# Two conditioned feed-forward layers: new layout and queue order for the inputs, basis products ahead of the weight's transpositions

## The chip, the cores and the metric

The kernel runs on one core of one Trainium2 chip. The metric is the device time of one execution in microseconds (us); three runs of the kernel before gave 230.68, 230.73 and 230.92, median 230.73. Engines are called by the profile's names: PE is TensorE (PEld its weight loads), DVE is VectorE, ACT ScalarE, POOL GpSimd, SP SyncE.

## The reference

Two layers, each a per-sample channel mixing followed by a feed-forward product and a residual sum. `x` is 128 samples of 32 channels by 512.

```python
def mixed(x, kind, weights):            # weights[kind]: 32x32 for each sample
    return jnp.einsum('bct,bcd->bdt', x, weights[kind])

# layer 0
base = einsum('bsd,od->bso', y, W_base) + b_base
e0, e1 = einsum('bsd,rd->bsr', y, enc0), einsum('bsd,rd->bsr', y, enc1)      # ranks 32 and 8
w0, w1 = coefs0 * mask0, coefs1 * mask1                                      # 3 experts, [3, 512, rank]
decoded = einsum('bsr,eor->ebso', e0, w0) + einsum('bsr,eor->ebso', e1, w1)
update = real_fourier_orthogonal_multiply(decoded).sum(axis=0)               # an inverse real FFT
x = x + base + update * 0.5
# layer 1
x = x + scale * einsum('bsi,if->bsf', y, kernel * 2.0 - 1.0)
```

## The kernel before

A tile is four samples, 128 partitions of 512 columns; there are 32 tiles. Layer 0's base weight, encoder, decoder and Fourier basis are folded into one 512x512 matrix before the first tile. This stage ahead of the loop is what the change touches.

- The masked coefficients of the three experts are multiplied and summed on DVE (`masked`, `pair`, `decode`).
- PE multiplies `decode` with the even and odd halves of the Fourier basis (`basis_sb`, line 426), into `y1_ps` (odd) and `f1_ps` (even). ACT and DVE make `spectrum` out of the two.
- PE transposes the base weight `w_sb` into the four PSUM banks `a_ps` (`turn_w`, line 414: 16 transpositions of 128x128, eight per half), and adds the products of encoder and spectrum there (line 488).
- ACT and DVE split each bank into `a_high` and `a_low`.
- POOL computes the gather's indices from `row_of` (DVE, from `kinds`), gathers each sample's mixing rows, and ACT expands them into block diagonals (`blocks`, line 277).
- Then 32 tiles run through a software pipeline: mixing product (line 432), feed of layer 0 (452, 462), mixing, feed of layer 1 (469, 474), with residual sums on DVE and the bias on POOL.

Every engine runs its own program in the order in which it is written, and semaphores join them. Loads are issued by SP and ACT (hardware queues q1 and q10 in the profile) and POOL (software queue q0), each queue in the order of its issues. The weight comes in two halves, one from SP, one from ACT. Before the first real product PE runs products of a zero tile (`warm_up`, line 407), ten, and two more after the first eight transpositions.

Of the kernel before, what the change touches and what calls it, by code (L numbers as in the profile page):

```python
# [23 lines left out]
P = 128  # L24
SAMPLES, C, T = 128, 32, 512
PER_TILE = P // C
TILES = SAMPLES // PER_TILE
CHUNKS = T // P
KINDS0, KINDS1 = 16, 32
EXPERTS, R0, R1 = 3, 32, 8  # L30
R = R0 + R1
HALF = T // 2 + 1
SCALING = 16.0 / 32.0
LAYERS = 2
# [20 lines left out]
    return np.ascontiguousarray(f.reshape(P, CHUNKS // 2, 2, HALF).transpose(2, 0, 1, 3).astype(np.float32))  # L55


def build(nc, x, kind0, kind1, mix0, w_base, b_base, enc0, enc1, coefs0, coefs1, mask0, mask1,
          mix1, sign_bits, scale, basis, out):
    f32, f32r, u8 = mybir.dt.float32, mybir.dt.float32r, mybir.dt.uint8  # L60
    i32, u32 = mybir.dt.int32, mybir.dt.uint32
    ALU, ACT = mybir.AluOpType, mybir.ActivationFunctionType
# [7 lines left out]
    with ctx:  # L70
        def sb(name, shape, dt):
            return ctx.enter_context(nc.sbuf_tensor(name, shape, dt))
# [4 lines left out]
        def sem(name):  # L77
            return ctx.enter_context(nc.semaphore(name))


        kinds = sb("kinds", [P, LAYERS, SAMPLES], i32)
        channel = sb("channel", [P, 1], i32)
        partition = sb("partition", [P, 1], i32)
        row_of = sb("row_of", [P, TILES, LAYERS], i32)
# [4 lines left out]
        w_sb = sb("w_sb", [P, CHUNKS, T], f32)  # L89
        basis_sb = sb("basis_sb", [P, 2, CHUNKS // 2, HALF], f32)  # L90

        coefs_sb = sb("coefs_sb", [P, EXPERTS, CHUNKS * R], f32)
        masks_sb = sb("masks_sb", [P, EXPERTS, CHUNKS * R], u8)
# [4 lines left out]
        enc_sb = sb("enc_sb", [P, T], f32)  # L98
# [30 lines left out]
        kinds_loaded, partition_ready, channel_ready, row_of_ready = (  # L129
            sem("kinds_loaded"), sem("partition_ready"), sem("channel_ready"), sem("row_of_ready"))  # L130
        blocks_zero, idle_zero = sem("blocks_zero"), sem("idle_zero")
        w_loaded = [sem(f"w_loaded{half}") for half in range(2)]
        basis_loaded = [sem(f"basis_loaded{parity}") for parity in range(2)]
        coefs_loaded, masks_loaded = sem("coefs_loaded"), sem("masks_loaded")
        enc_loaded, bits_loaded, bias_loaded, scale_loaded = (
            sem("enc_loaded"), sem("bits_loaded"), sem("bias_loaded"), sem("scale_loaded"))
        ident_zero, ident_ready = sem("ident_zero"), sem("ident_ready")
# [19 lines left out]


        def load_w(queue, half):
            part = slice(half * T // 2, (half + 1) * T // 2)  # L160
            queue.dma_start(w_sb[:, :, part], w_base.rearrange("(c p) d -> p c d", p=P)[:, :, part]).then_inc(w_loaded[half], 16)

        @block.sync
        def _(sp):
            sp.dma_start(kinds[:, 0, :], kind0.partition_broadcast(P)).then_inc(kinds_loaded, 16)  # L165
            load_w(sp, 0)
            sp.dma_start(coefs_sb[:, :, CHUNKS * R0:], coefs1.rearrange("e (p q) r -> p e (q r)", q=CHUNKS)).then_inc(coefs_loaded, 16)
            sp.dma_start(basis_sb[:, 1], basis[1]).then_inc(basis_loaded[1], 16)
            sp.wait_ge(enc_zero, 1)
            sp.dma_start(enc_sb[0:R0, :], enc0).then_inc(enc_loaded, 16)  # L170
            sp.dma_start(enc_sb[R0:R, :], enc1).then_inc(enc_loaded, 16)
            sp.dma_start(bias[:, :], b_base.partition_broadcast(P)).then_inc(bias_loaded, 16)
            sp.dma_start(x_in[:, 1, :], x_tiles[1]).then_inc(x_loaded[1], 16)
            sp.dma_start(bits_sb[:, :, :], sign_bits.rearrange("(c p) f -> p c f", p=P)).then_inc(bits_loaded, 16)
            sp.dma_start(scale_sb[:, :], scale.partition_broadcast(P)).then_inc(scale_loaded, 16)
            sp.dma_start(x_in[:, 2, :], x_tiles[2]).then_inc(x_loaded[2], 16)

            def load(tile, slot):
                sp.wait_ge(mixed0, tile - RING + 1)
                sp.wait_ge(biased, tile - RING + 1)  # L180
                sp.dma_start(x_in[:, slot, :], x_tiles[bass.ds(tile, 1)].rearrange("a p t -> (a p) t")
                             ).then_inc(x_loaded[slot], 16)

            def store(tile, slot):
                sp.wait_ge(out_ready, tile + 1)
                sp.dma_start(out_tiles[bass.ds(tile, 1)].rearrange("a p t -> (a p) t"), x1[:, slot, :]
                             ).then_inc(stored[slot], 16)

            looped = (TILES - RING) // RING * RING
            with sp.Fori(0, looped, RING) as base:  # L190
                for u in range(RING):
                    load(base + u + RING, u)
                    store(base + u, u)
            for tile in range(looped, TILES - 1):
                if tile + RING < TILES:
                    load(tile + RING, tile % RING)
                store(tile, tile % RING)
            for half, columns in enumerate(halves):
                sp.wait_ge(out_ready, TILES + half)
                sp.dma_start(out_tiles[TILES - 1][:, columns], x1[:, (TILES - 1) % RING, columns]).then_inc(ended, 16)  # L200

            for slot in range(RING):
                sp.wait_ge(stored[slot], 16 * len(range(slot, TILES - 1, RING)))
            sp.wait_ge(ended, 32)

        @block.gpsimd
        def _(pool):
            pool.dma_start(masks_sb[:, :, 0:CHUNKS * R0], mask0.rearrange("e (p q) r -> p e (q r)", q=CHUNKS)).then_inc(masks_loaded, 16)
            pool.dma_start(masks_sb[:, :, CHUNKS * R0:], mask1.rearrange("e (p q) r -> p e (q r)", q=CHUNKS)).then_inc(masks_loaded, 16)
            nc.gpsimd.iota(partition[:, :], pattern=[[0, 1]], base=0, channel_multiplier=1).then_inc(partition_ready, 1)  # L210

            nc.gpsimd.memset(ident[:, :], 0.0).then_inc(ident_zero, 1)
# [32 lines left out]
                if more:  # L245
                    gather(row_now[:, slot, :], slot)

            pool.wait_ge(row_of_ready, PER_TILE)
            gather(row_of[:, 0, :], 0)
            for slot in range(1, RING):  # L250
                gather(row_of[:, slot, :], slot)
# [8 lines left out]

        @block.scalar
        def _(act):
            act.dma_start(kinds[:, 1, :], kind1.partition_broadcast(P)).then_inc(kinds_loaded, 16)
            act.dma_start(coefs_sb[:, :, 0:CHUNKS * R0], coefs0.rearrange("e (p q) r -> p e (q r)", q=CHUNKS)).then_inc(coefs_loaded, 16)
            act.dma_start(basis_sb[:, 0], basis[0]).then_inc(basis_loaded[0], 16)
            load_w(act, 1)
            act.dma_start(x_in[:, 0, :], x_tiles[0]).then_inc(x_loaded[0], 16)
# [46 lines left out]
        def _(dve):  # L314
# [4 lines left out]
            dve.wait_ge(partition_ready, 1)  # L319
            nc.vector.tensor_scalar(channel[:, :], partition[:, :], C - 1, None, ALU.bitwise_and).then_inc(channel_ready, 1)  # L320
            dve.wait_ge(channel_ready, 1)
            dve.wait_ge(kinds_loaded, 16 * LAYERS)
            for j in range(PER_TILE):
                part = slice(j * C, (j + 1) * C)
                nc.vector.tensor_scalar(row_of[part, :, :].rearrange("p n l -> p l n"), kinds[part, :, j::PER_TILE], float(C), channel[part, :],
                                        ALU.mult, ALU.add).then_inc(row_of_ready, 1)

            dve.wait_ge(coefs_loaded, 32)
            dve.wait_ge(masks_loaded, 32)
            nc.vector.tensor_tensor(out=masked[:, :, :], in0=coefs_sb[:, :, :], in1=masks_sb[:, :, :], op=ALU.mult).then_inc(masked_ready, 1)  # L330
            dve.wait_ge(masked_ready, 1)
            nc.vector.tensor_tensor(out=pair[:, :], in0=masked[:, 0, :], in1=masked[:, 1, :], op=ALU.add).then_inc(pair_ready, 1)
# [2 lines left out]
            for first, rank, at in ((0, R0, 0), (CHUNKS * R0, R1, R0)):  # L335
                part = slice(first, first + CHUNKS * rank)
                nc.vector.tensor_tensor(out=decode[:, :, at:at + rank], in0=pair[:, part].rearrange("p (q r) -> p q r", r=rank),
                                        in1=masked[:, 2, part].rearrange("p (q r) -> p q r", r=rank), op=ALU.add).then_inc(decode_ready, 1)

            dve.wait_ge(odd_ready, 1)  # L340
            nc.vector.tensor_scalar(constant2[:, :], odd_part[:, 0:1], 2.0, None, ALU.mult).then_inc(constant_ready, 1)
# [60 lines left out]
        def _(pe):  # L402

            pe.wait_ge(idle_zero, 1)
            def warm_up(count):
                for _ in range(count):
                    nc.tensor.matmul(f0_ps[:, :], idle[:, 0:P], idle[:, :], start=True, stop=True)  # L407


            def turn_w(half):  # L410
                pe.wait_ge(w_loaded[half], 16)
                for k in (2 * half, 2 * half + 1):
                    for c in range(CHUNKS):
                        nc.tensor.matmul(a_ps[k][:, c * P:(c + 1) * P], w_sb[:, c, k * P:(k + 1) * P], ident[:, :],  # L414
                                         start=(c == 0), stop=False, is_transpose=True, skip_group_check=True)

            warm_up(10)
            pe.wait_ge(ident_ready, 1)
            turn_w(0)
            warm_up(2)  # L420

            pe.wait_ge(decode_ready, 2)
            for parity, to, done in ((0, odd_ps, odd_done), (1, even_ps, even_done)):
# [47 lines left out]
            def feed1_low(count, to=f1_ps[:, :], columns=slice(0, T)):  # L471
# [3 lines left out]
                                            start=False, stop=(k == CHUNKS - 1))  # L475
                last.then_inc(fed1, 1)

            turn_w(1)

            pe.wait_ge(enc_loaded, 32)  # L480
            for k in range(CHUNKS):
                if k == FIRST_MIX:
                    mix0_tile(0, 0, 0)
# [39 lines left out]
                feed1_low(TILES, end_ps[half], halves[half])  # L523


INPUTS = ["x", "itok_B_0_15", "itok_B_0_30", "L0_cond_weights", "L0_ffn_W_base", "L0_ffn_b_base", "L0_ffn_enc0",
          "L0_ffn_enc1", "L0_ffn_coefs0", "L0_ffn_coefs1", "L0_ffn_mask0", "L0_ffn_mask1", "L1_cond_weights",
          "L1_ffn_kernel", "L1_ffn_scale"]


# [13 lines left out]
```

## Time and profile before

| | |
|---|---|
| median of three runs | 230.73 us |
| span of the profiled execution | 229.0 us |
| time around the span, median less span | 1.7 us |
| PE busy | 221.5 us, 97% |
| DVE, ACT, POOL busy | 99.7, 75.1, 111.6 us |
| chain that ended last | PE 95%, DMA 3% |

The profiled execution has no time of its own but its span; 1.7 us is the distance of the median to it. A span is from the first to the last instruction. A busy share says how much of the span an engine's instructions took; the chain that ended last says what the end waited for, step by step.

### The profile page before, as it was taken

The numbers are of one execution on the slowest core, as the hardware profiler recorded it, in microseconds if no ns is written. First come the engines' busy times: TensorE is split into PE (matmuls) and PEld (weight loads), VectorE is DVE, ScalarE is ACT, GpSimd is POOL, SyncE is SP. The second block draws the span as 40 slices with busy tenths as digits, with TensorE's granted clock in tenths as the row PEclk, the third lists the DMA queues.
The fourth block names the chain that finished last, engine by engine and source line by source line (L and its number), as shares of the span: only waits on it lengthen the run. The fifth ranks groups of instructions, "written<-read, shape, count | busy, mean of one in ns | idle before, by whom it ended". The sixth has DMA issues, their size and how long they took to land.

```text
span 229.0 us, 3592 instructions
## 1 busy us (share of the span) xinstructions
PE 221.5 (97%) x1206; PEld 185.7 (81%) x1206; DVE 99.7 (44%) x150; ACT 75.1 (33%) x199; POOL 111.6 (49%) x135
## 2 busy tenths in 40 slices
PE   7499999999999999999999999999999999999995
PEld 2376888888888888888888888888888888888884
DVE  2325634434343434434343434434344444434334
ACT  0228433322333233322333333322333333322211
POOL 5466834555545444555545445555545444522200
PEclk9999999999999999999999999999999999999999
DMA  2972032123323322223322331223323232123112
GB/s 43 315 254 52 9 93 72 69 66 94 97 94 97 97 80 73 78 67 94 97 95 97 97 94 58 77 69 94 97 94 97 97 88 71 69 67 92 46 46 93
DMA packets 14789, 20.51 MB, mean 90 GB/s; under 512 B 2808, under 2 KB 6280, under 8 KB 14784
## 3 DMA queue, kind: packets, MB, share of 16 engines
q1 hardware_dynamic: 11312, 18.03, 24.6%
q0 software_dynamic: 2112, 1.11, 2.4%
q10 hardware_dynamic: 1360, 1.31, 2.0%
q8 instruction: 2, 0.03, 0.1%
q14 instruction: 3, 0.02, 0.0%
HBM read 12.06 MB, written 8.39 MB: 89 GB/s over the span
## 4 chain that ended last, share of the span: by engine, by line
PE 95%; DMA 3%; DVE 0%; issue 0%; SPq 0%
PE f_ps L452 26%; PE y_ps L432 25%; PE f_ps L462 13%; PE f_ps L474 13%; PE f_ps L469 13%; DMA w_sb<-in_L_ffn_W_base 3%; PE a_ps L488 2%; PE a_ps L414 1%; PE y_ps L426 1%; DVE x L398 0%; PE a_ps L469 0%; PE f_ps L426 0%; PE f_ps L407 0%; PE a_ps L474 0%; SPq L165 0%
## 5 line engine op out<-in xcount | busy, mean ns | idle before, releaser
L228 POOL TENSOR_TENSOR x<-x_in,bias 128x512 f32<-128x512 f32 x32 | 40.8, 1275 | 81.1 <-issue 46.6
L221 POOL DMA_INDIRECT gathered<-in_L_cond_weights,row_now x58 | 56.5, 973 | 13.2 <-issue 9.2
L452 PE MATMUL f_ps<-a_high,y_high 128*128 128x512 f32 x128 | 53.5, 418 | 0.0
L452 PE MATMUL f_ps<-a_low,y_high 128*128 128x512 f32 x128 | 50.4, 394 | 0.0
L364 DVE TENSOR_TENSOR x<-f_ps,x 128x512 f32<-128x512 f32 x32 | 22.1, 692 | 49.7 <-PE f_ps L452 48.1
L290 ACT ACTIVATE y_high<-y_ps 128x512 fp32r<-128x512 f32 x32 | 19.1, 597 | 69.4 <-PE y_ps L432 69.4
L286 ACT ACTIVATE y_high<-y_ps 128x512 fp32r<-128x512 f32 x32 | 19.1, 597 | 61.7 <-PE y_ps L432 59.7
L469 PE MATMUL f_ps<-b_sign,y_high 128*128 128x512 f32 x124 | 36.3, 414 | 0.0
L432 PEld LDWEIGHTS y_ps<-blocks,x_in 128*128 128x128 f32 x256 | 33.5, 191 | 3.3 <-issue 0.5
L432 PEld LDWEIGHTS y_ps<-blocks,x 128*128 128x128 f32 x256 | 33.3, 191 | 3.2 <-DVE x L364 0.5
L462 PE MATMUL f_ps<-a_high,y_low 128*128 128x512 f32 x128 | 35.0, 394 | 0.0
L277 ACT ACTIVATE blocks<-gathered 32x64 f32<-32x64 f32 x128 | 32.6, 255 | 4.5 <-issue 1.4
L474 PE MATMUL f_ps<-b_sign,y_low 128*128 128x512 f32 x124 | 34.0, 396 | 0.0
L432 PE MATMUL y_ps<-blocks,x 128*128 128x128 f32 x256 | 33.9, 275 | 0.0
L432 PE MATMUL y_ps<-blocks,x_in 128*128 128x128 f32 x256 | 33.7, 275 | 0.0
L357 DVE TENSOR_TENSOR y_low<-y_ps,y_high 128x512 fp32r<-128x512 f32 x32 | 22.1, 692 | 25.3 <-ACT y_high L290 23.0
L352 DVE TENSOR_TENSOR y_low<-y_ps,y_high 128x512 fp32r<-128x512 f32 x32 | 22.1, 692 | 23.0 <-ACT y_high L286 23.0
L370 DVE SCALAR_TENSOR_TENSOR x<-f_ps,scale_sb,x 128x512 f32<-128x512 f32 x31 | 23.3, 751 | 16.2 <-PE f_ps L474 15.7
L462 PEld LDWEIGHTS f_ps<-a_high,y_low 128*128 128x128 f32 x128 | 23.9, 187 | 5.9
L452 PEld LDWEIGHTS f_ps<-a_high,y_high 128*128 128x128 f32 x128 | 24.1, 188 | 4.7 <-issue 0.2
L452 PEld LDWEIGHTS f_ps<-a_low,y_high 128*128 128x128 f32 x128 | 24.1, 188 | 4.7 <-issue 0.2
L474 PEld LDWEIGHTS f_ps<-b_sign,y_low 128*128 128x128 f32 x124 | 23.2, 188 | 5.5
(46 smaller groups left out, 78.3 us busy)
## 6 DMA issues: line engine op xcount, KB each, us to landing
x_in<-in_x SPq DMA_DIRECT2D x31, 256.0 KB
out_x<-x SPq DMA_DIRECT2D x31, 256.0 KB, 2.0
gathered<-in_L_cond_weights,row_now POOLq DMA_INDIRECT x58
w_sb<-in_L_ffn_W_base SPq DMA_DIRECT2D x1, 512.0 KB
w_sb<-in_L_ffn_W_base ACTq DMA_DIRECT2D x1, 512.0 KB
basis_sb<-in_fourier_basis ACTq DMA_DIRECT2D x1, 257.0 KB
basis_sb<-in_fourier_basis SPq DMA_DIRECT2D x1, 257.0 KB
x_in<-in_x ACTq DMA_DIRECT2D x1, 256.0 KB
```

Of the source, the lines that this page charges most:

```text
L221: nc.gpsimd.indirect_dma_start(gathered[:, slot, layer, :], None, mix_rows[layer], IndirectOffsetOnAxis(rows[:, layer:layer + 1].bitcast(u ...
L228: nc.gpsimd.tensor_tensor(out=x1[:, slot, :], in0=x_in[:, slot, :], in1=bias[:, :], op=ALU.add).then_inc(biased, 1)
L277: nc.scalar.activation(blocks[part, slot, :, part], gathered[part, slot, :, :], ACT.Copy).then_inc(expanded, 1)
L352: nc.vector.tensor_tensor(out=y0_low[:, :], in0=y0_ps[:, :], in1=y0_high[:, :].bitcast(f32), op=ALU.subtract).then_inc(y0_low_ready, 1)
L357: nc.vector.tensor_tensor(out=y1_low[:, :], in0=y1_ps[:, :], in1=y1_high[:, :].bitcast(f32), op=ALU.subtract).then_inc(y1_low_ready, 1)
L364: nc.vector.tensor_tensor(out=x1[:, slot, :], in0=f0_ps[:, :], in1=x1[:, slot, :], op=ALU.add).then_inc(x1_ready, 1)
L370: nc.vector.scalar_tensor_tensor(out=x1[:, slot, :], in0=f1_ps[:, :], scalar=scale_sb[:, 0:1], in1=x1[:, slot, :], op0=ALU.mult, op1=ALU.a ...
L432: last = nc.tensor.matmul(to[:, k * P:(k + 1) * P], of[:, k * P:(k + 1) * P], blocks[:, slot, layer, :], start=True, stop=True)
L452: last = nc.tensor.matmul(f0_ps[:, :], y0_high[:, k * P:(k + 1) * P], a[:, k, :], start=(k == 0 and a is a_high), stop=(k == CHUNKS - 1 an ...
L462: nc.tensor.matmul(f0_ps[:, :], y0_low[:, k * P:(k + 1) * P], a_high[:, k, :], start=False, stop=False)
L469: nc.tensor.matmul(to, y1_high[:, k * P:(k + 1) * P], b_sign[:, k, columns], start=(k == 0), stop=False)
L474: last = nc.tensor.matmul(to, y1_low[:, k * P:(k + 1) * P], b_sign[:, k, columns], start=False, stop=(k == CHUNKS - 1))
```

## The change

Host-side, the two sets of coefficients and masks become one array each, laid out so that every partition reads one contiguous row; the two encoders become one array, and the kinds become an array by partition, [128, 32, 2], with each sample's kind repeated for its 32 channels. So the two coefficient DMAs, two mask DMAs, two encoder DMAs and two kinds DMAs become one each. The halves of the base weight are by rows (output chunks) and not by columns. The queues' order changes. On PE, the idle products are 18 and run together, the basis products come next, and all sixteen transpositions after them. The numbers in the kernel's lines above are of the kernel before.

```diff
-            part = slice(half * T // 2, (half + 1) * T // 2)
-            queue.dma_start(w_sb[:, :, part], w_base.rearrange("(c p) d -> p c d", p=P)[:, :, part]).then_inc(w_loaded[half], 16)
+            part = slice(2 * half, 2 * half + 2)
+            queue.dma_start(w_sb[:, part, :], w_base.rearrange("(c p) d -> p c d", p=P)[:, part, :]).then_inc(w_loaded[half], 16)
@@ SP
-            sp.dma_start(kinds[:, 0, :], kind0.partition_broadcast(P)).then_inc(kinds_loaded, 16)
+            sp.dma_start(coefs_sb[:, :, :], coefs).then_inc(coefs_loaded, 16)
+            sp.dma_start(basis_sb[:, 1], basis[1]).then_inc(basis_loaded[1], 16)
             load_w(sp, 0)
-            sp.dma_start(coefs_sb[:, :, CHUNKS * R0:], coefs1.rearrange("e (p q) r -> p e (q r)", q=CHUNKS)).then_inc(coefs_loaded, 16)
-            sp.dma_start(basis_sb[:, 1], basis[1]).then_inc(basis_loaded[1], 16)
             sp.wait_ge(enc_zero, 1)
-            sp.dma_start(enc_sb[0:R0, :], enc0).then_inc(enc_loaded, 16)
-            sp.dma_start(enc_sb[R0:R, :], enc1).then_inc(enc_loaded, 16)
+            sp.dma_start(enc_sb[0:R, :], enc).then_inc(enc_loaded, 16)
@@ POOL
-            pool.dma_start(masks_sb[:, :, 0:CHUNKS * R0], mask0.rearrange("e (p q) r -> p e (q r)", q=CHUNKS)).then_inc(masks_loaded, 16)
-            pool.dma_start(masks_sb[:, :, CHUNKS * R0:], mask1.rearrange("e (p q) r -> p e (q r)", q=CHUNKS)).then_inc(masks_loaded, 16)
@@ ACT
-            act.dma_start(kinds[:, 1, :], kind1.partition_broadcast(P)).then_inc(kinds_loaded, 16)
-            act.dma_start(coefs_sb[:, :, 0:CHUNKS * R0], coefs0.rearrange("e (p q) r -> p e (q r)", q=CHUNKS)).then_inc(coefs_loaded, 16)
+            act.dma_start(kinds[:, :, :], kinds_in).then_inc(kinds_loaded, 16)
+            act.dma_start(masks_sb[:, :, :], masks).then_inc(masks_loaded, 16)
@@ DVE
-            for j in range(PER_TILE):
-                part = slice(j * C, (j + 1) * C)
-                nc.vector.tensor_scalar(row_of[part, :, :].rearrange("p n l -> p l n"), kinds[part, :, j::PER_TILE], float(C), channel[part, :],
-                                        ALU.mult, ALU.add).then_inc(row_of_ready, 1)
+            nc.vector.tensor_scalar(row_of[:, :, :], kinds[:, :, :], float(C), channel[:, :], ALU.mult, ALU.add).then_inc(row_of_ready, 1)
@@ PE
-                for k in (2 * half, 2 * half + 1):
-                    for c in range(CHUNKS):
+                for k in range(CHUNKS):
+                    for c in (2 * half, 2 * half + 1):
-            warm_up(10)
-            pe.wait_ge(ident_ready, 1)
-            turn_w(0)
-            warm_up(2)
+            warm_up(18)
...
+            pe.wait_ge(ident_ready, 1)
+            turn_w(0)
             turn_w(1)
-            pe.wait_ge(enc_loaded, 32)
+            pe.wait_ge(enc_loaded, 16)
```

PE before, from its first product to the encoder's last (`f0_ps<-idle` are the idle products, `y1_ps` and `f1_ps` the basis products, `a_ps<-ident,w_sb` the transpositions):

```order
L407 MATMUL f0_ps<-idle 128x512 x10
L414 MATMUL a_ps0<-ident,w_sb 128x128 x4
L414 MATMUL a_ps1<-ident,w_sb 128x128 x4
L407 MATMUL f0_ps<-idle 128x512 x2
L426 MATMUL y1_ps<-basis_sb,decode 128x257 x2
L426 MATMUL f1_ps<-basis_sb,decode 128x257 x2
L414 MATMUL a_ps2<-ident,w_sb 128x128 x4
L414 MATMUL a_ps3<-ident,w_sb 128x128 x4
L488 MATMUL a_ps0<-spectrum,enc_sb 128x257
```

PE now, the same stretch:

```order
L401 MATMUL f0_ps<-idle 128x512 x18
L417 MATMUL y1_ps<-basis_sb,decode 128x257 x2
L417 MATMUL f1_ps<-basis_sb,decode 128x257 x2
L408 MATMUL a_ps0<-ident,w_sb 128x128 x2
L408 MATMUL a_ps1<-ident,w_sb 128x128 x2
L408 MATMUL a_ps2<-ident,w_sb 128x128 x2
L408 MATMUL a_ps3<-ident,w_sb 128x128 x2
...
L481 MATMUL a_ps0<-spectrum,enc_sb 128x257
```

The basis products moved ahead of all transpositions, and each half of the weight now fills two chunks of all four banks, where it filled two banks whole.

SP's queue before, its first loads (shapes are partitions by elements of a row):

```order
L165 DMA kinds<-in_itok_B_15 128x128
L161 DMA w_sb<-in_L_ffn_W_base 128x4x256
L167 DMA coefs_sb<-in_L_ffn_coefs 128x3x32
L168 DMA basis_sb<-in_fourier_basis 128x514
L170 DMA enc_sb<-in_L_ffn_enc 32x512
L171 DMA enc_sb<-in_L_ffn_enc 8x512
L172 DMA bias<-in_L_ffn_b_base 128x512
```

SP's queue now:

```order
L165 DMA coefs_sb<-in_coefs 128x480
L166 DMA basis_sb<-in_fourier_basis 128x514
L161 DMA w_sb<-in_L_ffn_W_base 128x2x512
L169 DMA enc_sb<-in_enc 40x512
L170 DMA bias<-in_L_ffn_b_base 128x512
```

The coefficients and the basis moved ahead of SP's half of the weight, and the kinds left this queue.

ACT's queue now (before it was kinds, the larger part of the coefficients, basis, weight, x):

```order
L259 DMA kinds<-in_kinds 128x64
L260 DMA masks_sb<-in_masks 128x480
L261 DMA basis_sb<-in_fourier_basis 128x514
L161 DMA w_sb<-in_L_ffn_W_base 128x2x512
L263 DMA x_in<-in_x 128x512
```

The masks came here from POOL's software queue, and the coefficients went to SP.

## Rows read from the trace of the kernel before

**Rows 1.** The page: span, PE's busy time, shares of the last chain.

```profile
span 229.0 us, 3592 instructions
PE 221.5 (97%) x1206; PEld 185.7 (81%) x1206; DVE 99.7 (44%) x150; ACT 75.1 (33%) x199; POOL 111.6 (49%) x135
PE 95%; DMA 3%; DVE 0%; issue 0%; SPq 0%
```

**Rows 2.** Busy us (instructions) by stretch: PE, PEld, DVE, ACT, POOL; clock, DMA share, GB/s.

```profile
190.00:209.50 19.50, 19.50 (x110) 16.77 (x109) 8.48 (x12) 6.80 (x19) 7.71 (x8) 1.00 0.28 85
```

**Rows 3.** The last chain before the loop: start us, us, what.

```profile
1.20 7.50 DMA w_sb<-in_L_ffn_W_base
9.01 1.94 PE a_ps L414 x8
10.95 0.85 PE f_ps L407 x2
11.80 1.95 PE y_ps L426 x4
13.75 0.93 PE f_ps L426 x4
14.82 1.09 PE a_ps L414 x8
15.91 1.73 PE a_ps L488 x6
17.64 0.89 PE y_ps L432 x8
```

**Rows 4.** Timeline of PE: start us, us, instructions, idle before and releaser.

```profile
1.21 4.45 PE L407 MATMUL f_ps<-idle 128*128 128x512 bf16 x10 [1.21 <-DVE idle L315]
9.01 1.94 PE L414 MATMUL a_ps<-ident,w_sb 128*128 128x128 f32 x8 [3.35 <-DMA w_sb<-in_L_ffn_W_base]
```

**Rows 5.** Timeline of POOL's first mask DMA and DVE's instructions around it.

```profile
1.29 0.93 POOL L208 DMA_DIRECT2D masks_sb<-in_L_ffn_mask  x1 [0.83 <-POOLq L535]
10.17 0.66 DVE L330 TENSOR_TENSOR masked<-coefs_sb,masks_sb 128x480 f32<-128x480 f32 x1 [2.04 <-DMA masks_sb<-in_L_ffn_mask]
11.22 0.39 DVE L337 TENSOR_TENSOR decode<-pair,masked 128x128 f32<-128x128 f32 x2
15.14 0.41 DVE L348 SCALAR_TENSOR_TENSOR spectrum<-f_ps,mirrored 128x255 f32<-128x255 f32 x1
```

**Rows 6.** Timeline of row_of, the first gather and its expansion.

```profile
6.97 1.17 DVE L325 TENSOR_SCALAR row_of<-kinds,channel 32x64 int32<-32x64 int32 x4 [3.55 <-DMA kinds<-in_itok_B]
8.41 1.03 POOL L221 DMA_INDIRECT gathered<-in_L_cond_weights,row_of  x1 [4.11 <-DVE row_of L325]
15.55 1.09 ACT L277 ACTIVATE blocks<-gathered 32x64 f32<-32x64 f32 x4 [1.38 <-issue]
```

**Rows 7.** Busy time by stretch, before and after 5.5 us.

```profile
0.00:5.50 5.50, 4.29 (x10) 1.34 (x10) 1.61 (x4) 0.02 (x1) 2.97 (x10) 1.00 0.21 38
5.50:15.00 9.50, 6.01 (x21) 4.21 (x21) 3.16 (x11) 1.86 (x3) 5.07 (x6) 1.00 1.07 324
```

**Rows 8.** DMA queues (packets, MB, share), windows 0:5.5, 0:8, 0:13; the kinds' landing (us).

```profile
q1 hardware_dynamic: 214, 0.15, 12.5%
q10 hardware_dynamic: 124, 0.06, 8.8%
...
q1 hardware_dynamic: 912, 0.63, 28.2%
...
q1 hardware_dynamic: 1633, 1.54, 40.3%
q10 hardware_dynamic: 1162, 1.04, 29.2%
q0 software_dynamic: 64, 0.06, 1.4%
...
kinds<-in_itok_B ACTq DMA_DIRECT2D x1, 64.0 KB, 5.0
```

More of the change, by code:

```diff
@@ L55, in fourier_basis, with build @@
     return np.ascontiguousarray(f.reshape(P, CHUNKS // 2, 2, HALF).transpose(2, 0, 1, 3).astype(np.float32))
-def build(nc, x, kind0, kind1, mix0, w_base, b_base, enc0, enc1, coefs0, coefs1, mask0, mask1,
+def build(nc, x, kinds_in, mix0, w_base, b_base, enc, coefs, masks,
           mix1, sign_bits, scale, basis, out):
@@ L78, in sem @@
             return ctx.enter_context(nc.semaphore(name))
-        kinds = sb("kinds", [P, LAYERS, SAMPLES], i32)
+        kinds = sb("kinds", [P, TILES, LAYERS], i32)
         channel = sb("channel", [P, 1], i32)
@@ L246, in prepare @@
                     gather(row_now[:, slot, :], slot)
-            pool.wait_ge(row_of_ready, PER_TILE)
+            pool.wait_ge(row_of_ready, 1)
             gather(row_of[:, 0, :], 0)
@@ L321, in _ @@
             dve.wait_ge(channel_ready, 1)
-            dve.wait_ge(kinds_loaded, 16 * LAYERS)
-            for j in range(PER_TILE):
-                part = slice(j * C, (j + 1) * C)
-                nc.vector.tensor_scalar(row_of[part, :, :].rearrange("p n l -> p l n"), kinds[part, :, j::PER_TILE], float(C), channel[part, :],
-                                        ALU.mult, ALU.add).then_inc(row_of_ready, 1)
-            dve.wait_ge(coefs_loaded, 32)
-            dve.wait_ge(masks_loaded, 32)
+            dve.wait_ge(kinds_loaded, 16)
+            nc.vector.tensor_scalar(row_of[:, :, :], kinds[:, :, :], float(C), channel[:, :], ALU.mult, ALU.add).then_inc(row_of_ready, 1)
+            dve.wait_ge(coefs_loaded, 16)
+            dve.wait_ge(masks_loaded, 16)
             nc.vector.tensor_tensor(out=masked[:, :, :], in0=coefs_sb[:, :, :], in1=masks_sb[:, :, :], op=ALU.mult).then_inc(masked_ready, 1)
@@ L523, in _, with by_partition, kinds_by_partition @@
                 feed1_low(TILES, end_ps[half], halves[half])
-INPUTS = ["x", "itok_B_0_15", "itok_B_0_30", "L0_cond_weights", "L0_ffn_W_base", "L0_ffn_b_base", "L0_ffn_enc0",
-          "L0_ffn_enc1", "L0_ffn_coefs0", "L0_ffn_coefs1", "L0_ffn_mask0", "L0_ffn_mask1", "L1_cond_weights",
-          "L1_ffn_kernel", "L1_ffn_scale"]
+INPUTS = ["x", "kinds", "L0_cond_weights", "L0_ffn_W_base", "L0_ffn_b_base", "enc", "coefs", "masks",
+          "L1_cond_weights", "L1_ffn_kernel", "L1_ffn_scale"]
+def by_partition(per_rank0, per_rank1):
+    sides = [np.asarray(a).reshape(EXPERTS, P, -1) for a in (per_rank0, per_rank1)]
+    return np.concatenate(sides, axis=2).transpose(1, 0, 2)
+def kinds_by_partition(kind0, kind1):
+    both = np.stack([np.asarray(k).reshape(TILES, PER_TILE) for k in (kind0, kind1)], axis=2)
+    return np.repeat(both.transpose(1, 0, 2), C, axis=0)
 def kernel(**inputs):
@@ L535 @@
     nc = bacc.Bacc("TRN2", target_bir_lowering=False, num_devices=1)
+    inputs["kinds"] = kinds_by_partition(inputs["itok_B_0_15"], inputs["itok_B_0_30"])
+    inputs["enc"] = np.concatenate([inputs["L0_ffn_enc0"], inputs["L0_ffn_enc1"]])
+    inputs["coefs"] = by_partition(inputs["L0_ffn_coefs0"], inputs["L0_ffn_coefs1"])
+    inputs["masks"] = by_partition(inputs["L0_ffn_mask0"], inputs["L0_ffn_mask1"])
     arrays = {name: np.ascontiguousarray(inputs[name]) for name in INPUTS}
```

## The prediction

> **What bounds the kernel now.** I read the page first. PE is busy 97% of the span, the chain that ended last is 95% PE and 3% one DMA [rows 1]. A stretch late in the loop has PE busy for 19.50 of 19.50 us [rows 2], so the 31 steps of the main loop have no gap, and this change touches none of their instructions. What can move the end is the stage before the loop, and a microsecond saved on PE there should arrive at the end whole. So I read that stage in the chain, in order of time [rows 3]: a DMA until 8.70 (half 0 of the base weight), then PE alone. The first eight transpositions take 1.94 us, two idle products 0.85, the four pieces of the odd basis product 1.95, the even ones 0.93, the other eight transpositions 1.09, then the encoder products, the first mixing product and feed.
>
> Then the inputs of each step. PE ran ten idle products from 1.21 to 5.66 and then rested until 9.01 for the weight [rows 4]. VectorE waited 2.04 us for the masks, which landed at 10.17 though GpSimd had issued them at 1.29; masked, pair and decode end at 11.61 [rows 5]. So the basis product could not start before about 11.7 in any case: the weight and then the masks bound this stretch. The kinds reached VectorE at 6.97, the gathers were issued from 8.41 and ScalarE could expand the first only at 15.55 [rows 6]. The DMA engines moved 38 GB/s up to 5.5 us, 324 GB/s from there to 15 [rows 7], and the two hardware queues' shares are in [rows 8].
>
> The span, 229.0 us, is of one execution; the median of the timed runs is 230.73, so 1.7 us lie around the span. I add up in the span and carry the difference over to the median. About 0.2% (0.46 us) is what a measurement of this kernel can tell from no change.
>
> **The change, part by part.** The new order on PE is 18 idle products, basis products, sixteen transpositions, encoder. The encoder products began in the chain at 15.91 [rows 3]; the question is when the sixteen transpositions end now, and how far ahead of 15.91 that is.
>
> *Idle products.* Ten ran 1.21 to 5.66, 0.427 us apart by two of them in 0.85 us [rows 3, 4]. Eighteen at that pace end at 1.21 + 7.7 = 8.9. PE's clock shows in the same rows: eight transpositions took 1.94 us and later eight took 1.09, the odd basis product 1.95 and the even one 0.93 [rows 3]. The slower of each pair is at 1.2 GHz, the faster at 2.4, and the clock rose around 13.7, after PE had worked on from 9.01. (The granted clock prints as 1.00 in the early window too [rows 7]; the durations tell more.) With unbroken work from 1.21 I expect it to rise between 5.7, which it had not done in ten, and 8; if it rises at 6.9, 13 products are done and the other five take half of 2.1, so the 18 end at 7.9. Bounds: 7.9 and 8.9.
>
> *Decode.* Masks and coefficients are now one contiguous row per partition, first in the queues. On SP 0.246 MB of coefficients, 0.263 of basis, 0.524 of weight: 1.033 MB. On ACT 0.033 kinds, 0.061 masks, 0.263 basis, 0.524 weight: 0.881 MB, then x. From 5.5 to 13 q1 moved 1.39 MB, 0.185 per us, and q10 0.98 MB, 0.131 per us [rows 8]. Half 0 of the weight, which ends at 0.59 MB on q1 behind the kinds, passed about 7.8 (0.63 MB by 8.0), was seen landed at 8.70, and PE started at 9.01 [rows 3, 8]: 0.9 from bytes to landing, 1.2 to PE. Now two bounds. Slow start: as before, only 0.15 and 0.06 MB by 5.5. Then the coefficients are through at 6.0, the masks at 5.8, decode inputs at 6.9; masked to decode took 10.17 to 11.61, 1.44 us [rows 5], so decode at 8.4, and basis 0 at 5.5 + 0.30/0.131 + 0.9 = 8.7. Fast start: the full rates from 2.0 (an estimate: SP issued its weight at 1.20 [rows 3], and something passes before bytes move), so decode some 3 us sooner. Either way the odd basis product starts at 8 to 9, not 11.7, and with the clock up both end near 10 to 10.9 (0.93 + 0.93 after 8.1 to 9.0). The spectrum followed the even product's end (14.68) by 0.86, at 15.55; now it is ready by 11.8, in the shadow of the transpositions, so it costs nothing; if the transpositions were to end before it, it would cost the difference. The two idle products between (0.85) are gone from the path.
>
> *The weight.* It now stands behind the basis. Slow: SP's half through at 5.5 + 0.883/0.185 = 10.3, at PE 11.5; ACT's at 5.5 + 0.82/0.131 = 11.8, at PE 13.0. The first eight transpositions hide in the wait for the second half; the last eight end at 13.0 + 1.09 = 14.1. Fast: 0.65 and 0.46 MB are through by 5.5, SP's half is at PE 8.8, ACT's at 9.9; PE, free at 9.8, does sixteen in 2.18 and ends at 12.0. So the encoder starts 1.8 us sooner (slow) to 3.9 us sooner (fast). Which end? Up to 5.5 the rows show 214 and 124 packets [rows 8], most of them the kinds, where 128 partitions read one row of 512 B. The new kernel starts with a row for each partition, of 256 to 2056 B. If packets were the limit, as many of the new ones carry about 0.45 MB where the old ones carried 0.21; if the shared row was, the start is fast. I take the middle of the two ends, 2.9 us.
>
> *The rest.* Encoder data are one DMA for two, behind SP's weight: 0.08 MB, 0.4 us, hidden by the transpositions. Four row_of instructions of 0.27 become one; kinds were on VectorE at 6.97 and POOL's gather started at 8.41. Now the kinds are a quarter as many bytes on one queue; 5.0 us to landing was the better of the two before [rows 8], so row_of at 5.8 and gather at 6.4 (1.44 behind the kinds before, with 0.9 of it the three instructions saved). The first gather took 15.55 − 8.41 = 7.1 us to expand, so 13.5 now, expanded at 14.6. It is wanted by the mixing product 1.73 us after the encoder starts, 14.7 to 15.8: just hidden. x is wanted at the same place; ACT's queue reaches its end at 1.143 MB, slow 13.8, landed 14.7: hidden. POOL loses two DMA issues, the first of 0.93 [rows 5], and zeroes the encoder tile earlier; SP waits for that before it issues the encoder, bias, x and bits, none of which is near its deadline. Everything from the encoder on keeps its distances. Sum: 229.0 − 2.9 = 226.1 in the span, about 230.7 − 2.9 = **227.9 us**.
>
> **The rivals.** *Queues at full rate from the start* (15%): the rows before don't show a start without the shared rows, so it can't be excluded. Gain 3.9: 226.9. For it: the first DMA of ACT's queue was 64 KB and took 5.0 us to land [rows 8], at 38 GB/s in all where later 324 were moved [rows 7]. DMA: Bandwidth & Descriptors (the Trainium skill, section on the anatomy of one DMA) gives about 2.0 us plus bytes over 436 GB/s for one; by that formula 64 KB take some 2.2 us, where this trace has 5.0, and the kernel would be at the fast end, so the trace disagrees with it as it stands.
>
> *The gathers bind* (12%). By 13.0 q0 had moved 0.06 MB, no more than the masks' 60 KB [rows 8], though the first gather had been issued at 8.41 [rows 6]: its bytes came with the end of the bulk. If they still come only then and ScalarE expands from 15.55, done at 16.64 [rows 6], the mixing product starts at 16.7 where it stood at 17.64: gain 0.9, 229.8. In part of these cases they come half a microsecond sooner: 229.3.
>
> *The clock falls in the wait for the weight* (10%), the way to the other side. PE has finished the basis products by 10 to 10.9 and rests up to 11.5 and again before 13.0. After the 3.35 us of rest before it worked at 1.2 GHz from 9.01 to 13.7 [rows 3, 4]. If the same happens here, 4.7 us of work go at half speed and 2.35 us are lost: 227.9 becomes 230.2, and from the slow end 231.3. It makes the kernel slower as soon as the second half reaches PE after 12.5 (12.5 + 1.09 + 2.35 = 15.9). Against it: these rests are some 1 us and 0.4 us, and nothing in the trace shows a clock that fell once it was up. TensorE: Matmul & The Clock Gate (the Trainium skill, on oscillation) warns of bursts separated by waits on DMAs, each starting cold; no row here shows such a fall.
>
> *The change gives nothing* (5%): its gain is eaten elsewhere before the loop, for instance by ScalarE's evictions of a_high: 230.7.
>
> **How the numbers follow.** Main case 58% (its own range 227.1 to 229.0, the bounds of the weight), fast start 15%, gathers 12%, clock 10% of which half slower, nothing 5%. The range 226.7 to 229.5 leaves out the clock case, no gain and the worse gathers, under 2 in 10. Faster: 58 + 15 + 12 + 3 = 88%; same 7%; slower 5%.
>
> **What would show it.** The idle products end at 7.9 to 8.9 with a halved pace at the end; decode ready by 8.5, the odd basis product from 8 to 9 in 0.93; a wait of PE for w_sb of 0.5 to 2 us, then transpositions at 1.09 for eight; encoder 12.0 to 14.1; the loop's stretches still at 19.50 of 19.50. Wrong would make me: transpositions at 1.94, a mixing product that waits for blocks, or a loop with gaps because x or its stores come too late.

## The result, and the profile after

The changed kernel takes 227.69 us (227.64 to 228.27 in four runs) against 230.82 before in the same runs; the ratio is 0.986, 95% interval 0.984 to 0.988. The forecast was 227.9, with a range of 226.7 to 229.5. The span fell by 3.5 us, from 229.0 to 225.5; the time by 3.1, since what lies around the span (median less span) grew from 1.8 to 2.2 us.

The page of the changed kernel, to be held against [rows 1]: the span, PE's busy time, and the last chain, by line.

```profile
span 225.5 us, 3597 instructions
PE 220.1 (98%) x1212; PEld 185.2 (82%) x1212; DVE 98.8 (44%) x147; ACT 75.0 (33%) x199; POOL 110.1 (49%) x133
PE f_ps L443 26%; PE y_ps L423 26%; PE f_ps L453 13%; PE f_ps L460 13%; PE f_ps L465 13%; DMA basis_sb<-in_fourier_basis 3%; PE a_ps L481 2%; PE a_ps L408 1%; PE y_ps L417 0%; DVE x L392 0%; PE a_ps L460 0%; PE f_ps L417 0%; PE a_ps L465 0%; ACTq L260 0%; ACTq L259 0%
```

PE is still the chain; the one DMA in it is now the basis, not the weight, and PE never waits for the weight. The chain before the loop (start us, us, what), the counterpart of [rows 3]:

```profile
1.67 6.68 DMA basis_sb<-in_fourier_basis
8.35 0.14 issue
8.49 1.11 PE y_ps L417 x4
9.60 0.87 PE f_ps L417 x4
10.47 1.75 PE a_ps L408 x16
12.21 1.73 PE a_ps L481 x6
13.94 1.08 PE y_ps L423 x8
15.02 1.72 PE a_ps L481 x4
```

The encoder products start at 12.21 where they stood at 15.91: 3.70 us. The first mixing product, behind them, takes 1.08 us where it took 0.89, so 3.5 are left. They reach the end, since the loop is as tight as before (the busy time of a late stretch, as in [rows 2]):

```profile
190.00:209.50 19.50, 19.50 (x110) 16.80 (x109) 8.64 (x13) 6.50 (x18) 5.77 (x5) 1.00 0.26 86
```

The timeline of what stands ahead of the basis products, as in [rows 4, 5, 6]:

```profile
1.20 5.87 PE L401 MATMUL f_ps<-idle 128*128 128x512 bf16 x18 [1.20 <-DVE idle L311]
3.91 0.26 DVE L319 TENSOR_SCALAR row_of<-kinds,channel 128x64 int32<-128x64 int32 x1 [1.40 <-DMA kinds<-in_kinds]
4.45 1.11 POOL L217 DMA_INDIRECT gathered<-in_L_cond_weights,row_of  x1 [2.40 <-DVE row_of L319]
4.74 0.66 DVE L323 TENSOR_TENSOR masked<-coefs_sb,masks_sb 128x480 f32<-128x480 f32 x1 [0.58 <-DMA masks_sb<-in_masks]
5.80 0.39 DVE L330 TENSOR_TENSOR decode<-pair,masked 128x128 f32<-128x128 f32 x2
8.49 1.11 PE L417 MATMUL y_ps<-basis_sb,decode 128*128 128x257 f32 x4 [1.42 <-DMA basis_sb<-in_fourier_basis]
12.66 1.09 ACT L273 ACTIVATE blocks<-gathered 32x64 f32<-32x64 f32 x4 [2.64 <-DMA gathered<-in_L_cond_weights,row_of]
```

VectorE has the kinds at 3.9 us (before: 7.0) and `decode` is ready at 6.2 (before: 11.6). The idle products end at 7.07, and PE then rests 1.42 us for the basis half in ACT's queue, which the odd product needs. The first gather is issued 4 us sooner, but ScalarE starts to expand its rows only 2.9 us sooner and is done at 13.75, two tenths ahead of the product that wants them. The queues in the window 0:5.5 (packets, MB, share), against the first two of [rows 8]:

```profile
q1 hardware_dynamic: 436, 0.81, 47.6%
q10 hardware_dynamic: 378, 0.28, 15.5%
```

They moved 1.09 MB by 5.5 us where the kernel before moved 0.21.

### The profile page after: what moved, and what is told of

It reads as the page before. It is cut to its first block, busy times and chain, and to the rows that moved or that the text cites. A ratio compares the mean times of both kernels' runs of the same rounds, so it can differ in the third digit from the quotient of the medians.

```text
span 225.5 us, 3597 instructions
## 1 busy us (share of the span) xinstructions
PE 220.1 (98%) x1212; PEld 185.2 (82%) x1212; DVE 98.8 (44%) x147; ACT 75.0 (33%) x199; POOL 110.1 (49%) x133
## 4 chain that ended last, share of the span: by engine, by line
PE 95%; DMA 3%; DVE 0%; ACTq 0%; issue 0%
PE f_ps L443 26%; PE y_ps L423 26%; PE f_ps L453 13%; PE f_ps L460 13%; PE f_ps L465 13%; DMA basis_sb<-in_fourier_basis 3%; PE a_ps L481 2%; PE a_ps L408 1%; PE y_ps L417 0%; DVE x L392 0%; PE a_ps L460 0%; PE f_ps L417 0%; PE a_ps L465 0%; ACTq L260 0%; ACTq L259 0%
```

## The experiments

The open questions were which edit ended the slow start, whether PE's order or the loads bring the gain, and what the idle products are for. Times are medians; the kernel before, measured beside each group, had 230.97 to 231.09. Line numbers in rows are each kernel's own.

**Only the kinds new.** The kernel before, with the kinds' array by partition, and with it the one `row_of` instruction for four:

```diff
-            sp.dma_start(kinds[:, 0, :], kind0.partition_broadcast(P)).then_inc(kinds_loaded, 16)
...
-            act.dma_start(kinds[:, 1, :], kind1.partition_broadcast(P)).then_inc(kinds_loaded, 16)
+            act.dma_start(kinds[:, :, :], kinds_in).then_inc(kinds_loaded, 16)
```

> The kernel before with only the kinds changed: one array with a row of 256 bytes for each partition, loaded by ACT, one row_of instruction; SP starts with its half of the weight. Theory (the shared rows of the kinds make the slow start): 0.6 MB or more by 5.5 us in place of 0.21, SP's weight landed near 6.5 in place of 8.7, masks and decode 1 to 2 us sooner, time 229 to 229.8. Rival (the slow start has another cause, such as the masks in the software queue or the many short rows): near 0.3 MB by 5.5 and 230.5 or more.

Measured: 228.92 us (227.86 to 230.02), ratio 0.990, interval 0.985 to 0.995. Queues in the window 0:5.5, then the timeline of DVE and PE, then busy time by stretch (the third number from the end is the granted clock):

```profile
q1 hardware_dynamic: 936, 0.59, 35.5%
q10 hardware_dynamic: 664, 0.46, 25.3%
q0 software_dynamic: 16, 0.03, 1.8%
...
8.21 0.66 DVE L326 TENSOR_TENSOR masked<-coefs_sb,masks_sb 128x480 f32<-128x480 f32 x1 [3.87 <-DMA masks_sb<-in_L_ffn_mask]
9.71 2.08 PE L422 MATMUL y_ps<-basis_sb,decode 128*128 128x257 f32 x4 [2.43 <-DVE decode L333]
...
5.50:9.00 3.50, 1.79 (x11) 1.28 (x9) 0.75 (x2) 0.00 (x0) 2.59 (x4) 1.00 1.05 332
9.00:12.00 3.00, 2.29 (x5) 1.85 (x6) 0.62 (x3) 0.17 (x1) 2.39 (x3) 0.60 1.06 318
```

1.08 MB in 5.5 us, in 1616 packets, with the masks still in the software queue and the short rows of coefficients still there. So the kinds' loads alone made the slow start, and this edit alone takes about 2 us off, at the lower edge of what was expected. It can take more: in the profiled run (229.58, the second slowest) the masks come at 8.21, PE rests 2.43 us, and its clock falls to half (0.60 of full on average from 9 to 12). The two quicker runs of the four, 227.86 and 228.26, have a mean granted clock of 1.00, and the quickest is as fast as the changed kernel. In these two most of the change's gain is there by this one edit.

**Only the kinds old.** The changed kernel, with the two kinds loads of before, each first in its queue, and the four row_of instructions.

```diff
+            sp.dma_start(kinds[:, 0, :], kind0.partition_broadcast(P)).then_inc(kinds_loaded, 16)
...
-            act.dma_start(kinds[:, :, :], kinds_in).then_inc(kinds_loaded, 16)
+            act.dma_start(kinds[:, 1, :], kind1.partition_broadcast(P)).then_inc(kinds_loaded, 16)
```

> The changed kernel with only the kinds as before: two loads of one shared 512-byte row each, first in SP's and ACT's queue, and four row_of instructions. Theory (the shared rows of the kinds are the slow start): 0.2 to 0.3 MB by 5.5 us in place of 1.09, decode about 8.5, the odd basis product from about 10, encoder at 14 or later, 229.7 to 230.5 with the clock up and more if PE's rest brings it down. Rival (new rows for the other inputs and their order do most): 228.3 or less.

Measured: 229.94 (229.88 to 230.14), ratio 0.995, interval 0.993 to 0.997. Window 0:5.5 of the queues, then the timeline of ACT and PE:

```profile
q1 hardware_dynamic: 191, 0.16, 10.7%
q10 hardware_dynamic: 149, 0.07, 8.0%
...
15.23 0.81 ACT L274 ACTIVATE blocks<-gathered 32x64 f32<-32x64 f32 x3 [4.34 <-DMA gathered<-in_L_cond_weights,row_of]
...
16.46 0.79 PE L427 MATMUL y_ps<-blocks,x_in 128*128 128x128 f32 x5 [1.45 <-ACT blocks L274]
```

The slow start is back at 0.23 MB, and 2.1 us of the gain are gone, as the theory had it. The way was in part another: the encoder starts at about 13.3 and not at 14 or later, a loss of 1.1, but the gathers wait for the kinds and then PE for the blocks, 1.45 us more. All other edits together are worth 1.0 us here.

**A shared row, and rows of their own.** To the changed kernel one load of 64 KB more at the head of each hardware queue, into a tile that nothing reads. In the first kernel all partitions read the same 512 bytes of the bias (two adjacent pieces for the two queues), in the second each reads a row of its own, of x. The first kernel's edit:

```diff
+            sp.dma_start(extra[:, 0, :], b_base[0*P:0*P+P].partition_broadcast(P)).then_inc(extra_loaded[0], 16)
...
+            act.dma_start(extra[:, 1, :], b_base[1*P:1*P+P].partition_broadcast(P)).then_inc(extra_loaded[1], 16)
```

> The changed kernel with one more load first in SP's and in ACT's queue, 64 KB each into a tile that nothing reads, every partition reading the same 512 bytes of the bias. Theory (the slow start before came from many partitions reading one short row): the queues start slowly again, about 0.2 to 0.3 MB by 5.5 us in place of 1.09, the encoder products start at 14 and not 12.2, time about 229.5. Rival (what counts is only how many bytes and packets stand ahead): 0.13 MB more at about 0.3 MB per us, 0.4 us later, about 228.1.

> The same two extra loads of 64 KB and 512-byte rows, but each partition reads a row of its own (of x). Both theories: 0.4 us later than the changed kernel, about 228.1, with about 0.95 MB or more moved by 5.5 us. If this one is slow too, the shared row is not the cause.

Measured: 229.11 (229.01 to 229.28) and 228.23 (227.86 to 228.84); ratios to before 0.992 (0.991 to 0.994) and 0.988 (0.986 to 0.989). Busy time 0:5.5 of the first, then its first DMAs' time to landing, and the same of the second:

```profile
0.00:5.50 5.50, 4.30 (x12) 1.63 (x13) 1.47 (x4) 1.49 (x2) 1.23 (x8) 1.00 0.44 117
...
extra<-in_L_ffn_b_base ACTq DMA_DIRECT2D x1, 64.0 KB, 4.4
```

```profile
0.00:5.50 5.50, 4.30 (x13) 1.62 (x14) 1.72 (x5) 1.49 (x2) 1.79 (x9) 1.00 0.57 164
...
extra<-in_x ACTq DMA_DIRECT2D x1, 64.0 KB, 2.3
```

The same bytes in the same shape land in 2.3 us with rows of their own and in 4.4 with a shared one, and the kernel is 0.9 us slower. So the sharing does cost. The same 128 KB with rows of their own cost at most 0.5 us against the changed kernel, and the intervals overlap, so bytes and packets alone are not what held up the start before. But the size was a miss: 0.64 MB moved by 5.5 us where 0.2 to 0.3 was expected (0.90 with own rows), and 117 GB/s is not 38. The two shared rows of the bias slow the start less than the two kinds arrays did. What the kinds' case has beyond it stays open; that the two arrays lay worse for each other in memory is possible and wasn't tried.

**PE's order alone.** The kernel before, with 18 idle products, then basis products, then both halves' transpositions.

```diff
-            warm_up(10)
-            turn_w(0)
-            warm_up(2)
+            warm_up(18)
...
+            turn_w(0)
             turn_w(1)
```

> The kernel before with only PE's order changed: 18 idle products, basis products when decode is there, then all sixteen transpositions. Theory (the gain is the loads'; PE's order alone can't bring it): PE rests from 7 to 9 until decode at 11.6; the basis products start at 11.7 and the encoder at 15.3 with the clock up (230.1) or at about 17 with the clock down again after the rest (231.5). Rival (PE's order and the idle products bring most of it): 228.5 or less.

Measured: 232.66 (231.89 to 233.28), ratio 1.006, interval 1.004 to 1.009: slower, by more than the 231.5 of the theory. PE's timeline, and the busy time by stretch with the clock:

```profile
11.70 2.08 PE L423 MATMUL y_ps<-basis_sb,decode 128*128 128x257 f32 x4 [3.64 <-DVE decode L337]
...
8.10:11.70 3.60, 0.00 (x0) 0.00 (x0) 1.38 (x4) 0.00 (x0) 2.72 (x3) 0.81 1.08 301
11.70:15.00 3.30, 3.30 (x8) 2.65 (x9) 0.51 (x2) 0.39 (x1) 2.39 (x4) 0.50 1.08 346
```

The clock was up at 8.1; in the rest of 3.64 us it fell to 0.50 of full, which is 1.2 GHz, and basis products and part of the transpositions ran at half speed. `decode` came no sooner than before (11.6), so nothing stood against this loss.

**The loads alone.** The changed kernel with PE's order of before (ten idle products, SP's eight transpositions, two idle, basis products, the other eight): the diff above the other way round.

> The changed kernel with PE's order of before: ten idle products, eight transpositions of SP's half, two idle products, basis products, eight transpositions. Theory (the loads bring most of the gain, PE's order places the transpositions behind what lands first): PE waits for the weight landed at 9.2, then 0.9 to 1.9, 0.4 to 0.9, 1.9 to 2.9 and 0.9 us: encoder at 13.5 with the clock up, 14.8 with it down after the rest from 5.6; 229.0 to 230.2. Rival (PE's order doesn't matter with the loads early): 227.9.

Measured: 230.89 (ten runs, 228.23 to 231.45), ratio 0.997, interval 0.993 to 1.000. A miss for theory and rival: I had 229.0 to 230.2, or 227.9. The profile is of one of the quickest runs, 228.50. PE's timeline and busy time by stretch:

```profile
7.42 1.90 PE L408 MATMUL a_ps<-ident,w_sb 128*128 128x128 f32 x8 [2.49 <-DMA w_sb<-in_L_ffn_W_base]
...
5.50:9.00 3.50, 1.58 (x8) 1.61 (x9) 0.52 (x3) 0.00 (x0) 2.67 (x3) 0.78 0.99 290
9.00:12.00 3.00, 3.00 (x12) 2.25 (x11) 0.09 (x1) 0.39 (x1) 2.15 (x3) 0.69 1.08 360
```

Even in this one the clock falls, behind a rest of 2.49 us: the weight stands later in the queue than the old order of PE wants. So all the new loads without PE's order give nothing clear of noise, PE's order without the loads loses, and both together give 3.1 us. The kinds' load by itself, under PE's old order, did better (228.92) than all the new loads under it (230.89): there SP's weight still stood first, and PE had it at 5.5 us and not at 7.4.

**Ten idle products, and 24**, in place of 18 in the changed kernel:

```diff
-            warm_up(18)
+            warm_up(10)        # second kernel: warm_up(24)
```

> The changed kernel with ten idle products in place of 18: PE is done with them at about 5.3 and rests until the odd basis data at 8.35, some 3 us. Theory (a rest of 2.5 us or more lets the clock fall and several us of work then go at half speed): odd, even products and part of the transpositions at the slow rate in most executions, 229 to 230.5, with a wide spread. Rival (eight idle products only fill time): 227.7.

> The changed kernel with 24 idle products: they fill the rest of 1.4 us before the odd basis data where the clock has risen by 5, and end at 8.4 to 9.5 where it rises at 5 to 6.5. Theory (18 is enough; a rest of 1.4 us costs nothing but its own time): 227.7 to 228.3, no better than 18. Rival (the short rest still costs clock in some executions): 227.3 and less spread.

Measured, with ten: 228.32 (ten runs, 227.08 to 230.41), ratio 0.990, interval 0.986 to 0.993. With 24: 227.59 (227.08 to 228.19), ratio 0.986, interval 0.982 to 0.989. With ten, three runs end at 227.1 to 227.3, three at 228.1 to 228.5 and four at 229.8 to 230.4, so the median lies between theory and rival. The profile is of the quickest run:

```profile
1.20 4.45 PE L401 MATMUL f_ps<-idle 128*128 128x512 bf16 x10 [1.20 <-DVE idle L311]
7.77 1.11 PE L417 MATMUL y_ps<-basis_sb,decode 128*128 128x257 f32 x4 [2.12 <-DMA basis_sb<-in_fourier_basis]
```

The ten idle products ran at half speed throughout (4.45 us, as in the kernel before), and behind the rest of 2.12 us the odd product ran at full speed (1.11 us). So here the clock did not hold over the rest; it came up by the end of it. Of the other runs only the mean granted clock is on record: 0.992 in 228.10, 228.09, 228.54, 229.76 and 229.82, which is the value of the profiled kernels whose clock fell for a while, and 1.00 in the two slowest, 229.88 and 230.41. Those two could have got the clock late, since the figure also reads 1.00 over idle products at half speed; that is not shown. 24 can't be told from 18, and its median lies between its theory and its rival.

**What bounds next.** Four variants of the changed kernel: the basis loads exchanged between SP and ACT; both basis loads on SP (and none on ACT); SP waiting for the first gathered rows ahead of bias, x and sign bits; and this wait together with both basis loads on SP. The added lines of the fourth, with the basis line that was there already:

```diff
+            sp.dma_start(basis_sb[:, 0], basis[0]).then_inc(basis_loaded[0], 16)
             sp.dma_start(basis_sb[:, 1], basis[1]).then_inc(basis_loaded[1], 16)
...
+            sp.wait_ge(rows_gathered[0], 16 * LAYERS)
             sp.dma_start(bias[:, :], b_base.partition_broadcast(P)).then_inc(bias_loaded, 16)
```

> The changed kernel with the two basis loads exchanged: SP, whose basis landed at 4.5 us, brings the odd product's, ACT, whose basis landed at 8.35, the even one's. Odd product from about 7.1, even from 8.5 to 9.4. Theory (the gathered rows, expanded at 13.75, and the second half of the weight, landed at 11.05, stand right behind): encoder from about 12.0, first mixing product still from 13.8, gain at most 0.2 us, about 227.5. Rival (the basis alone bounds): the whole 1.0 us comes through, 226.7.

> The changed kernel with both basis halves on SP ahead of its weight, and no wait for the gathers. Theory (the weight's bytes now bound PE, and the gathers right behind it): transpositions from 9.6 to 10.5, encoder by 11.6 to 12.2, first mixing product waits for the blocks at 13 to 13.8; 227.0 to 227.7. Rival (gathers are not a bound once the basis is early): as the variant with the wait, 226.8 in its best execution.

> The changed kernel, SP waiting for the first tile's gathered rows before it issues bias, x and sign bits. Theory (the software queue gets its turn when the hardware queues run dry): gathered rows there by 11 in place of 12.66, the second half of the weight sooner too; the odd basis load at 8.35 still bounds the encoder at 12.2, so the first mixing product starts at 13.9 and the gain is 0.1 to 0.3 us, about 227.5. Rival (gathers take their time whatever the traffic): no sooner, 227.7. The risk: the later loads come too late, more than 228.5.

> The same with both basis halves on SP ahead of its weight, ACT with kinds, masks, weight, x. Theory (three things stand close together: ACT's slow basis, the weight's second half, the gathers; only with all three moved does PE gain): both weight halves landed by 9.5 to 10, idle products end at 7 to 8, basis products at 9 to 10, encoder at 11.0 to 11.5 in place of 12.2, blocks ready before 12.7: 226.5 to 227.0. Rival (the weight lands no sooner, since the bytes are the same): 227.7.

Measured: exchanged 228.09 (226.90 to 229.20); both on SP 228.73 (228.02 to 230.06); gathers first 227.54 (226.99 to 230.34); both edits 227.69 (226.76 to 228.01). Ratios 0.987 (0.983 to 0.992), 0.990 (0.985 to 0.995), 0.983 (0.980 to 0.986), 0.986 (0.983 to 0.988). None is told from the changed kernel as faster, and the expectations of the first and second were misses; the fourth came out at its rival's 227.7. PE's timeline of the exchanged one, then of both on SP with its busy time, then PE and ACT of gathers first with its busy time, then ACT of both edits:

```profile
12.01 1.10 PE L408 MATMUL a_ps<-ident,w_sb 128*128 128x128 f32 x8 [0.60 <-DMA w_sb<-in_L_ffn_W_base]
```

```profile
10.44 3.20 PE L408 MATMUL a_ps<-ident,w_sb 128*128 128x128 f32 x16 [1.67 <-DMA w_sb<-in_L_ffn_W_base]
...
12.00:15.00 3.00, 3.00 (x13) 2.70 (x12) 0.00 (x0) 1.06 (x5) 1.52 (x3) 0.61 0.13 35
```

```profile
9.71 1.11 PE L418 MATMUL y_ps<-basis_sb,decode 128*128 128x257 f32 x4 [3.04 <-DMA basis_sb<-in_fourier_basis]
...
11.47 1.09 ACT L274 ACTIVATE blocks<-gathered 32x64 f32<-32x64 f32 x4 [0.23 <-DMA gathered<-in_L_cond_weights,row_of]
...
9.00:12.00 3.00, 2.29 (x8) 1.91 (x9) 0.59 (x2) 0.89 (x3) 2.17 (x3) 0.82 0.20 63
```

```profile
10.35 1.09 ACT L274 ACTIVATE blocks<-gathered 32x64 f32<-32x64 f32 x4 [1.24 <-DMA gathered<-in_L_cond_weights,row_of]
```

With the odd basis early the wait passes to the weight, and in the second kernel the clock fell behind that wait: sixteen transpositions in 3.20 us, where the changed kernel's timeline has 1.91. My expectation of 227.0 to 227.7 for it had no clock in it, but that is not all: its two runs with a granted clock of 1.00 took 228.02 and 228.19. The profile of gathers first is of its slowest run, 230.34. The odd product behind the rest of 3.04 us still ran at full speed (1.11 us), and the clock fell at about 10.9 (an estimate from the 0.82 above), some 1.2 us after PE had gone on; the other four runs, 226.99 to 227.75, have a granted clock of 1.00.

With SP holding back, the gathered rows are there at 11.47 and 10.35. The fair comparison is not only the changed kernel's 12.66: with ten or 24 idle products, the basis exchanged or both on SP they came at 12.01 to 12.10. So 0.5 to 1.7 us are won, which speaks for the gathers being held up by the bulk. In its best execution the combined kernel takes 226.76, with the encoder at 11.55, near the best of the others (226.90, 226.99).

## Why the prediction was right, and where its terms were off

The time and the place of the gain were forecast rightly; the state of the queues at the start, and with it what PE would wait for, was not, and two errors of size met in the number.

- *What bounds.* PE's chain, the weight and then the masks before: right. A gain ahead of the encoder does reach the end: of the 3.70 us all but 0.2 came through. But the main case was bounded by the weight, with a wait of PE for it of 0.5 to 2 us as a sign. There was no such wait; the rest of 1.42 us was for ACT's basis.
- *Idle products* (7.9 to 8.9): ended at 7.07. I had the clock rise after 5.7, because ten had not seen it. In this run they sped up after ten; in the profiles of the variants the same eighteen took 5.47 to 6.95 us. The time of the rise is each execution's own.
- *The queues' start.* The middle of a slow and a fast start was wrong: it was the fast one (a rival at 15%). The reason stood in my own sentence, the kinds' load with its shared row. Two kernels that change only the kinds' loads show it (1.08 MB and 0.23 MB by 5.5 us); the shared row as such is shown to cost, but not to cost all of it.
- *Shares of the queues.* I gave SP 0.65 and ACT 0.46 MB by 5.5 in the fast case, at the rates of before. It was 0.81 and 0.28, with like numbers of packets, 436 and 378: ACT begins with rows of 256 and 480 bytes. So decode (some 3 us ahead of 8.4 in the fast case, 6.2 measured) was not the bound. The basis of ACT, which the same rates put near 5.6 in the fast case, landed at 8.35, and PE rested for it. That the odd product began at 8.49, inside the 8 to 9 that I gave, is luck in part: I had it wait for a slow decode and a slow basis. The fast case had the weight at PE at 8.8 and 9.9; it landed at 9.2 and 11.05, which stayed hidden, since PE came late.
- *The sum.* Middle 2.9 in the span; measured 3.5. I had 0.6 too little there, and took the time around the span as constant where it grew by 0.4. That the time came within 0.2 us of 227.9 is luck in part: the two cancel.
- *Clock in the wait.* In the profiled run it stayed up over 1.42 us of rest, and the transpositions ran 16 in 1.75. The mechanism that I gave 10% is real all the same: the profiles of five variants show it. My "nothing in the trace shows a clock that fell once it was up" held of the trace of before alone. The rule of the Trainium skill, TensorE: Matmul & The Clock Gate (on oscillation), that bursts between DMA waits start cold, agrees with the clock of 0.50 behind 3.64 us of rest, which was at bottom a wait for the masks' DMA. It does not fit the 3.04 us of waiting for the basis DMA with gathers first, behind which PE went on at full speed and slowed only later.
- *Gathers.* Right as to the place: hidden with 0.2 us to spare; bound in the variant with old kinds.
- *The formula of DMA: Bandwidth & Descriptors* (the Trainium skill, anatomy of one DMA). The page gives it for DMAs that GpSimd issues, which I left out; these were issued by SP and ACT. By it 64 KB take some 2.2 us (an estimate). The extra rows of their own landed in 2.2 and 2.3, the shared ones in 3.8 and 4.4, the kinds before in 5.0 and 6.1. It also says nothing of loads that stand behind others in a busy queue: the 257 KB of ACT's basis took 6.7 from their issue.

## What to carry to other kernels

Look at the bytes that the queues move in the first microseconds: a few small broadcast loads at their head, every partition reading one short row, can hold up all that stands behind them, and laying the row out by partition beforehand, though it is more data in memory, is the cheaper load. Moving TensorE's work and moving its inputs belong together: PE's new order over the old loads lost 1.6 us, and all the new loads under PE's old order gained nothing clear of noise, because PE then waited at another place and lost its clock behind the wait. Test the parts one by one as well: the kinds' load alone brought 2 of the 3 us. Before filling or opening a rest of PE, count what half speed would cost behind it, and profile more than one execution, since the clock is not the same in each, and compare an arrival with more than one run before calling it moved.

## What the runs showed of the hardware

- Two loads of 64 KB of one shared 512-byte row each, at the head of both queues, held all DMAs to 0.21 MB in 5.5 us; with one load of 32 KB by partition 1.08 MB moved in the same time. In front of the changed kernel's loads, two loads of 64 KB left 0.64 MB with shared rows and 0.90 MB with own rows.
- The clock fell in or behind rests of 2.43, 2.49, 3.04 and 3.64 us, and behind one of 1.67, and stayed up over 1.42, 1.59, 2.04 and 2.20 us. Behind 3.04 it fell only some 1.2 us after PE had gone on. The length of the rest alone doesn't decide; what else does is open.
- The granted clock prints 1.00 from the start, also where the ten idle products take 4.45 us, which is half speed. In the first microseconds durations tell the clock, not this figure.
- The time around the span is 1.8 to 2.1 us in the kernels with the old kinds loads and 2.2 to 2.5 in all with the new array. Why is open; it takes 0.4 us of the gain.
- Of the gathers through the software queue, the first issued at 4.45, nearly nothing had moved by 10 us (6 packets), and the first rows came at 12.66; in variants with the same gathers they came at 12.01 to 12.10, and at 11.47 and 10.35 where SP held back 1 MB.
